# Order of the gate's second choice, the expert sums and the next tile's projections in a fused attention and expert layer

## The chip, the cores and the metric

One Trainium2 chip, one of its cores. The metric is the device time of one execution in microseconds. The kernel before has a median of 419.21 us over 3 runs (419.05 to 419.9).

## The reference, cut to what matters

4096 tokens (4 sequences of 1024) of width 128, all in float32. A linear attention with running sums and 16 heads of 8, then a layer norm, an FFN of 512 with gelu, a layer norm, a residual and layer norm, and then eight experts that share one FFN and differ by a low-rank term:

```python
q = sigmoid(heads(Wq, bq)); k = sigmoid(heads(Wk, bk)); v = heads(Wv, bv)
sink_in = normal / sum((q + EPS) * (cumsum(k) + EPS))
src_out = normal / sum((k + EPS) * (cumsum(q) + EPS))
cons_sink = sum((q + EPS) * (cumsum(k * src_out) + EPS)) / normal
cons_src = clip(sum((k + EPS) * (cumsum(q * sink_in) + EPS)) / normal, -1, 1)
src_comp = exp(cons_src) / cumsum(exp(cons_src)) * normal
kv = cumsum(k outer (v * src_comp))                    # along the tokens
x = (q * sink_in / normal) . kv * sigmoid(cons_sink)
h = layernorm(inputs + x @ Wo + bo)
attn = layernorm(h + gelu(h @ W1 + b1) @ W2 + b2)
x2 = layernorm(inputs + attn)
scores = softmax(x2 @ gate_w.T + gate_b); top_v, top_i = top_k(scores, 2)
for e in range(8):
    gate = count(top_i == e) * top_v.sum()
    inter = x2 @ wi.T + bi + (x2 @ lora_A[e].T) @ lora_B[e].T
    out += gate * (relu(inter) @ wo.T + bo)
out = layernorm(x2 + out)
```

## The kernel before, in words

The tokens are worked in 8 tiles of 512 (`TILES`, `TOK`), four groups of 128 tokens each (`SUB`). Every engine runs one program, written out by hand as a list of calls; semaphores alone tie the programs together, so on each engine an instruction that waits holds up all behind it. A call `step(Tile(s))` does a part of four tiles at once: a = s + 1 (its attention up to piece 3), b = s (the rest of its attention, h, FFN), c = s - 1 (x2, gate, first half of its experts) and d = s - 2 (second half, output). Step -1 and `second_step` come first, steps 1 to 7 follow, then `closing`. In steps 1 to 6 tile a exists, in steps 2 to 7 tile d does.

The attention of a tile (lines 943 to 1043, with PE's lines 327 to 406): `cumulate_q`, `cumulate_k` and two products give head sums on PE (`head_sums`), their inverses are spread by ACT and transposed by PE (`denominators_T`), and the same again gives the conserved sums, `cumulate_e` and `compensation_T`. Out of it comes `values` (DVE, vs = v times the factors, line 1030). SP spreads vs by eight DMAs (`spread_vs`, line 287), one for each piece m, with the eight rows of a head repeated; `outer_product(t, m)` multiplies piece m with k into one of three slots of kv, `cumulate_kv(t, m)` scans it, POOL's `product(t, m)` multiplies the scan with q_fac and PE's `reduce_out(t, m)` sums it up in pO. `q_fac` (`query_factor`) needs `factor_T` through bank pA.

The experts of tile c: `x2_T`, `logits`, `lora_in` (PE, bank pM), 13 small gate steps on DVE (`gate`, line 1068, each waits for the one before it), `masked_lora` (line 1121: u1 is the low-rank input under the first choice's mask, ud under second minus first), `u_T` (line 453: the transposes of u1 and ud on PE, both into pM), `u1T_out` and `udT_out` (ACT), and for each quarter f `inter_base`, `inter1` (with u1T), `relu` (ACT), `inter2` (adds udT's part), `second_relu` (DVE, the sum for both choices), `expert_out`. Quarters 0 and 1 are done in step c + 1, quarters 2 and 3 a step later, when the tile is called d.

ACT's order in the middle of a step is `u1T_out(c)`, `gated_constant(c)`, `seed_x(a)`, `udT_out(c)`, `normalise(d, 3)`, `relu(c, 0)`, `relu(c, 1)`, `normalise(b, 1)`. POOL's order over the end of a step is `product(a, 0)`, `scaled_n2(b)` (needs `normalise(b, 1)`, line 870), and in the next step, where that tile is c, `outer_residual` (line 876), two products, `inverse_std(c, 2)` and products 3 to 7. SP's order is spreads 0 and 1 of tile a, `store(d)` (needs `normalise(d, 3)`, line 294), spreads 2 and 3, and in the next step 4, 5, 6 and 7.

Two-input operations of DVE name their operands' homes in the rows: pA, pB, pO, pY, pG and pM are banks of PSUM, all else lies in SBUF.

Of the kernel before, what the change touches and what calls it, by code (L numbers as in the profile page):

```python
# [52 lines left out]
def wait(eng, sem, value):  # L53

    if value <= 0:
        return
    eng.wait_ge(sem, value)
# [8 lines left out]
def build(nc, x, x_t, att_w, consts, wo_rep, rows, gate_row, ffn_w, moe_w, out):  # L66
    ctx = ExitStack()
    with ctx:
# [136 lines left out]
        def u1_bank(t):  # L205
            return pO if t.n == TILES - 1 else pM
# [119 lines left out]
        def _(pe):  # L326
# [48 lines left out]
            def factor_T(t):  # L375
                pe.wait_ge(facx_ready, t.n + 1)
                pe.wait_ge(qsink_ready, t.n + 1)
                spread_T(pA, fac_x[:, :, :].rearrange("p a b -> p (a b)"), facT_ready)
# [74 lines left out]
            def u_T(t, first_one):  # L453
# [7 lines left out]
                elif first_one:  # L461
                    pe.wait_ge(u1_ready, t.n + 1)
                    pe.wait_ge(ud_ready, t.n + 1)
                else:
                    pe.wait_ge(u1T_ready, t.n + 1)
# [129 lines left out]
            def step(s):  # L595
# [3 lines left out]
                if s.n == 1:  # L599
                    pe.wait_ge(y_free[1], 16)  # L600
                    pe.wait_ge(cmoe_ready, 1)
                if D: inter_base(d, 2); inter1(d, 2); inter_base(d, 3); inter1(d, 3)
                if A: project_q(a)
                if s.n == 1: keep_busy(2, pM)
                if B: reduce_out(b, 1)
                if A: project_k(a)
# [24 lines left out]
                if B: ffn_out(b, 2); ffn_out(b, 3)  # L631
                if C: u_T(c, False)
                if A: factor_T(a)
                if C: inter_base(c, 0); inter1(c, 0); inter_base(c, 1); inter1(c, 1); inter2(c, 0); inter2(c, 1)
# [8 lines left out]
        def _(act):  # L643
# [152 lines left out]
            def step(s):  # L796
# [5 lines left out]
                if D: relu(d, 2)  # L802
                if A: q_out(a)
                if D: relu(d, 3)
                if A: k_out(a)
# [127 lines left out]
        def _(dve):  # L933
# [266 lines left out]
            def step(s):  # L1200
# [20 lines left out]
                if C: gate(c, 9)  # L1221
                if A: source(a); k_times_cum_q(a, 1); cumulate_source(a)
                if C: gate(c, 10)
                if A: q_times_cum_k(a, 1)
                if C: gate(c, 11)
                if D: expert_residual(d)
                if A: conserved(a); clip_source(a)
                if C: gate(c, 12); masked_lora(c, True)
                if A: prefix_e(a)
                if C: masked_lora(c, False)  # L1230
                if A: inverse_cum_e(a); source_factor(a); sink_factor(a)
                if D: piece_moments(d, 3)
                if A: values(a)
                if D: join_moments(d, 3)
                if B: moments(b, 1)
                if A: query_factor(a); outer_product(a, 0); cumulate_kv(a, 0)
                if A: outer_product(a, 1)
                if C: second_relu(c, 0); second_relu(c, 1)
                if A: outer_product(a, 2); cumulate_kv(a, 1); outer_product(a, 3); cumulate_kv(a, 2)
# [53 lines left out]
```

## Time and profile before

| | us |
|---|---|
| median of 3 runs | 419.21 (419.05 to 419.9) |
| the profiled execution | 418.39 |
| its span, first to last instruction | 416.6 |
| PE busy (matmul), weight loads | 374.6, 261.3 |
| DVE busy | 327.9 |
| ACT busy | 216.6 |
| POOL busy | 223.2 |
| mean granted clock of TensorE | 0.99 of full speed |
| chain that ended last | PE 31%, DVE 27%, POOL 19%, issue 14%, DMA 5% |

The shares are means over the start, six steps that look alike and a closing part. A step is read best by itself: the one taken here begins with DVE's `cumulate_q` at 178.56 and ends at 222.89. In it tile a is tile 4. PE is the matmul side; its times are modelled, so a busy PE needn't be at its peak. "Idle before" is the time in which an engine sat idle ahead of the instruction, and behind the arrow stands what ended it.

### The profile page before, as it was taken

What the parts mean: (1) busy time and instruction counts of PE and PEld (TensorE: products, weight loads), DVE (VectorE), ACT (ScalarE), POOL (GpSimd) and SP (SyncE); (2) the same over time, 40 slices, a digit from 0 to 9 for tenths busy, and PEclk for the clock granted to TensorE, in tenths of its full rate; (3) what the DMA queues carried; (4) which work ended last, traced back from release to release, by engine and by line L of the source; (5) the groups of instructions that cost most, each with busy time, mean ns of one, the idle gap of its engine ahead of it and who ended that gap; (6) DMA issues with size and microseconds to landing.
All of it is one profiled execution on the core that took longest, in us unless ns stands there. A gap on an engine that the chain in (4) does not pass through costs nothing.

```text
span 416.6 us, 6454 instructions
## 1 busy us (share of the span) xinstructions
PE 374.6 (90%) x2082; PEld 261.3 (63%) x2082; DVE 327.9 (79%) x787; ACT 216.6 (52%) x399; POOL 223.2 (54%) x263
## 2 busy tenths in 40 slices
PE   8897789788998999989998999899989997799991
PEld 3555556465756875677657774778478765775551
DVE  3649966599589988999799979997899889832632
ACT  2240226327853586538852795278644874175541
POOL 2017234983279527963497348942795369735211
PEclk9999999899999999999999999999999999999997
DMA  8236006400180007300560028000810063000000
GB/s 257 115 71 158 1 2 152 125 3 0 37 217 2 0 2 183 97 0 2 116 162 2 0 56 223 3 0 16 204 36 0 2 160 68 0 1 27 12 14 25
DMA packets 19857, 26.58 MB, mean 64 GB/s; under 512 B 1648, under 2 KB 9968, under 8 KB 19824
## 3 DMA queue, kind: packets, MB, share of 16 engines
q1 hardware_dynamic: 19680, 25.96, 24.5%
q8 instruction: 17, 0.28, 0.3%
q10 hardware_dynamic: 144, 0.21, 0.3%
q14 instruction: 16, 0.13, 0.1%
HBM read 7.29 MB, written 2.10 MB: 23 GB/s over the span
## 4 chain that ended last, share of the span: by engine, by line
PE 31%; DVE 27%; POOL 19%; issue 14%; DMA 5%; ACT 2%; SPq 0%; POOLq 0%; DVEq 0%; ACTq 0%
POOL prod L848 12%; PE pB L354 5%; DMA vb<-vs 5%; DVE kv L1037 5%; PE pY L428 4%; PE pG L421 3%; DVE cum_kv L1043 3%; DVE cum_ks L937 2%; PE pG L497 2%; POOL rstd L838 2%; PE pG L490 2%; DVE cum_q L937 2%; PE pY L508 2%; DVE cum_qs L937 2%; DVE gel L1141 2%
## 5 line engine op out<-in xcount | busy, mean ns | idle before, releaser
L848 POOL TENSOR_TENSOR prod<-cum_kv,q_fac 128x512 f32<-128x512 f32 x64 | 94.5, 1483 | 33.9 <-DVE cum_kv L1043 25.7
L404 PEld LDWEIGHTS pO<-s_wor,prod 128*128 128x128 f32 x512 | 62.2, 191 | 33.5 <-POOL prod L848 21.4
L404 PE MATMUL pO<-s_wor,prod 128*128 128x128 f32 x512 | 69.5, 281 | 14.0 <-POOL prod L848 13.9
L1037 DVE TENSOR_TENSOR kv<-k,vb 128x512 f32<-128x512 f32 x64 | 52.8, 825 | 6.7 <-DMA vb<-vs 6.7
L835 POOL TENSOR_TENSOR var_eps<-mv,s_con 128x4 f32<-128x4 f32 x32 | 9.9, 310 | 71.1 <-DVE mv L1063 71.1
L1043 DVE TENSOR_TENSOR_SCAN cum_kv<-p_ones,cum_kv,kv 128x512 f32<-128x512 f32 x32 | 40.5, 1275 | 0.6
L1043 DVE TENSOR_TENSOR_SCAN cum_kv<-p_ones,kv 128x512 f32<-128x512 f32 x32 | 38.5, 1213 | 0.5
L657 ACT ACTIVATE v<-pA,s_att 128x512 f32<-128x512 f32 x7 | 4.8, 687 | 62.9 <-PE pA L340 62.9
L754 ACT ACTIVATE relu<-pG,s_att 128x512 f32<-128x512 f32 x28 | 19.2, 684 | 27.4 <-PE pG L490 27.4
L508 PEld LDWEIGHTS pY<-s_moe,gel 128*128 128x128 f32 x256 | 30.7, 192 | 3.7 <-issue 1.9
L508 PE MATMUL pY<-s_moe,gel 128*128 128x128 f32 x256 | 32.6, 276 | 0.0
L838 POOL TENSOR_TENSOR rstd<-var_eps,s_con 128x4 f32<-128x4 f32 x32 | 32.5, 1014 | 0.0
L428 PE MATMUL pY<-s_ffn,gel 128*128 128x128 f32 x256 | 32.3, 276 | 0.0
L428 PEld LDWEIGHTS pY<-s_ffn,gel 128*128 128x128 f32 x256 | 30.4, 192 | 1.0 <-ACT pY L723 0.5
L421 PE MATMUL pG<-hT,s_ffn 128*128 128x512 f32 x64 | 30.5, 598 | 0.2
L484 PE MATMUL pG<-x2T,s_moe 128*128 128x512 f32 x60 | 30.6, 594 | 0.0
L490 PE MATMUL pG<-u1T,s_moe 128*128 128x512 f32 x60 | 30.5, 592 | 0.0
L497 PE MATMUL pG<-udT,s_moe 128*128 128x512 f32 x60 | 29.5, 605 | 0.0
L1141 DVE SCALAR_TENSOR_TENSOR gel<-pG,neg_bi,relu 128x512 f32<-128x512 f32 x28 | 20.3, 744 | 10.6 <-PE pG L497 10.5
L891 POOL TENSOR_TENSOR e_norm<-esrc,s_con 128x64 f32<-128x64 f32 x8 | 2.8, 346 | 40.8 <-ACT esrc L684 40.8
L354 PEld LDWEIGHTS pB<-s_att,kq 128*128 128x128 f32 x128 | 16.0, 191 | 12.5 <-issue 9.6
L712 ACT ACTIVATE gel<-pG,s_att 128x512 f32<-128x512 f32 x32 | 21.9, 685 | 2.8 <-PE pG L421 2.5
(164 smaller groups left out, 772.7 us busy)
## 6 DMA issues: line engine op xcount, KB each, us to landing
vb<-vs SPq DMA_DIRECT2D x64, 256.0 KB, 4.7
xT<-x_t SPq DMA_DIRECT2D x8, 256.0 KB, 4.3
xt<-x SPq DMA_DIRECT2D x8, 256.0 KB, 5.3
out<-y SPq DMA_DIRECT2D x8, 256.0 KB, 2.3
s_moe<-moe_w SPq DMA_DIRECT2D x1, 836.0 KB, 10.4
s_wor<-wo_rep SPq DMA_DIRECT2D x1, 512.0 KB, 8.2
s_ffn<-ffn_w SPq DMA_DIRECT2D x1, 512.0 KB, 8.9
s_con<-consts SPq DMA_DIRECT2D x1, 502.0 KB, 4.4
```

Source lines behind the costliest of these rows:

```text
L354: mm = pe.matmul(pB[:, end - P:end], src[:, s * P:(s + 1) * P], wide_sum, start=True, stop=True)
L404: mm = pe.matmul(pO3[:, s, :], prod[:, m % 4, s * P:(s + 1) * P], s_wor[:, m, :], start=False, stop=(m == DH - 1), skip_group_check=True)
L421: pe.matmul(pG[f % 2][:, :], w1[:, f * P:(f + 1) * P], hT[:, :], start=True, stop=True).then_inc(w1_done, 1)
L428: mm = pe.matmul(pY3[:, s, :], gel[:, f, s * P:(s + 1) * P], w2[:, f, :], start=False, stop=(f == FC - 1), skip_group_check=True)
L484: pe.matmul(expert_bank(t, f)[:, :], moe("wi")[:, f * P:(f + 1) * P], x2T[t.par][:, :], start=True, stop=False)
L490: pe.matmul(expert_bank(t, f)[:, :], moe("lb")[:, f * P:(f + 1) * P], u1T[:, :], start=False, stop=True).then_inc(in1_done, 1)
L497: pe.matmul(expert_bank(t, f)[:, :], moe("lb")[:, f * P:(f + 1) * P], udT[:, :], start=False, stop=True, skip_group_check=True).then_inc(i ...
L508: mm = pe.matmul(pY3[:, s, :], hsum[:, f, s * P:(s + 1) * P], wo[:, f, :], start=(f == 0 and s == 0), stop=(f == FC - 1), skip_group_check ...
L838: pool.tensor_tensor(rstd[i][:, :], var_eps[i][:, :], con("mhalf"), ALU.pow).then_inc(rstd_ready[i], 1)
L848: pool.tensor_tensor(prod[:, m % 4, :], cum_kv[t.par][:, m, :], q_fac[t.par][:, :], ALU.mult).then_inc(prod_ready, 1)
L1037: dve.tensor_tensor(kv[:, m % 3, :], k[t.par][:, :], vb[:, m, :], ALU.mult).then_inc(kv_ready, 1)
L1043: dve.tensor_tensor_scan(cum_kv[t.par][:, m, :], scan_ones, kv[:, m % 3, :], start, ALU.mult, ALU.add).then_inc(cumkv_ready, 1)
```

## The change

On DVE, gate step 9 goes from behind `cumulate_sink` to behind the moments of tile d, ahead of `values`; steps 10, 11 and 12 and ud's mask go behind `values`. The moments of d are joined earlier, `sink_factor` comes ahead of `source_factor`, and `cumulate_kv(a, 1)` ahead of the two `second_relu(c, ...)`. On PE, the first choice's transposes go into bank pA instead of pM, so they don't wait for ud any more but for q_sink of the tile two further on; `factor_T` waits for u1T, and stands with `inter_base(c, 0)` and `inter1(c, 0)` ahead of the transposes of ud. `project_q` and `project_k` stand at the head of a step, ahead of tile d's inner matmuls, and ACT's `q_out` and `k_out` ahead of its relus. The programs of SP and POOL are the same.

```diff
--- before.py
+++ after.py
@@ -203,7 +203,7 @@
             return prod[:, f, :] if t.n == TILES - 1 else relu1[:, f % 2, :]
 
         def u1_bank(t):
-            return pO if t.n == TILES - 1 else pM
+            return pO if t.n == TILES - 1 else pA
 
         p_den, p_cons, p_cume = pB[:, SUMS_AT:SUMS_AT + 2 * HW], pB[:, CONS_AT:CONS_AT + 2 * HW], pB[:, 0:HW]
         p_log = pM[:, LOG_AT:LOG_AT + SUB * EXPERTS].rearrange("p (s e) -> p s e", s=SUB)
@@ -375,6 +375,7 @@
             def factor_T(t):
                 pe.wait_ge(facx_ready, t.n + 1)
                 pe.wait_ge(qsink_ready, t.n + 1)
+                wait(pe, u1T_ready, t.n - 1)
                 spread_T(pA, fac_x[:, :, :].rearrange("p a b -> p (a b)"), facT_ready)
 
             def cumulate_e(t):
@@ -460,9 +461,12 @@
                         pe.wait_ge(ud_ready, t.n + 1)
                 elif first_one:
                     pe.wait_ge(u1_ready, t.n + 1)
+                    if t.plus(2).exists():
+                        pe.wait_ge(qsink_ready, t.n + 3)
+                    else:
+                        pe.wait_ge(qfac_ready, TILES)
+                else:
                     pe.wait_ge(ud_ready, t.n + 1)
-                else:
-                    pe.wait_ge(u1T_ready, t.n + 1)
                 for s in range(SUB):
                     mm = pe.transpose(dst[:, s * P:(s + 1) * P], src[:, s, :], ident)
                 mm.then_inc(done, 1)
@@ -599,11 +603,10 @@
                 if s.n == 1:
                     pe.wait_ge(y_free[1], 16)
                     pe.wait_ge(cmoe_ready, 1)
+                if A: project_q(a); project_k(a)
+                if s.n == 1: keep_busy(2, pM)
                 if D: inter_base(d, 2); inter1(d, 2); inter_base(d, 3); inter1(d, 3)
-                if A: project_q(a)
-                if s.n == 1: keep_busy(2, pM)
                 if B: reduce_out(b, 1)
-                if A: project_k(a)
                 if D: inter2(d, 2); inter2(d, 3)
                 if B: reduce_out(b, 2)
                 if s.n == 1: keep_busy(1, pM)
@@ -629,9 +632,10 @@
                 if B: ffn_out(b, 1)
                 if A: compensation_T(a)
                 if B: ffn_out(b, 2); ffn_out(b, 3)
+                if A: factor_T(a)
+                if C: inter_base(c, 0); inter1(c, 0)
                 if C: u_T(c, False)
-                if A: factor_T(a)
-                if C: inter_base(c, 0); inter1(c, 0); inter_base(c, 1); inter1(c, 1); inter2(c, 0); inter2(c, 1)
+                if C: inter_base(c, 1); inter1(c, 1); inter2(c, 0); inter2(c, 1)
                 if A: reduce_out(a, 0)
             opening(Tile(0))
             second_step(Tile(0))
@@ -799,10 +803,8 @@
                 A, B, C, D = a.exists(), b.exists(), c.exists(), d.exists()
                 if s.n == 1:
                     act.wait_ge(cmoe_ready, 1)
-                if D: relu(d, 2)
-                if A: q_out(a)
-                if D: relu(d, 3)
-                if A: k_out(a)
+                if A: q_out(a); k_out(a)
+                if D: relu(d, 2); relu(d, 3)
                 if C: normalise(c, 2); x2T_out(c)
                 if A: v_out(a)
                 if C: gate_exp(c)
@@ -1218,25 +1220,23 @@
                 if C: gate(c, 4); gate(c, 5); sum_exp(c)
                 if C: gate(c, 6); gate(c, 7); gate(c, 8); inverse_sum_exp(c); gate_total(c)
                 if A: sink(a); cumulate_sink(a)
-                if C: gate(c, 9)
                 if A: source(a); k_times_cum_q(a, 1); cumulate_source(a)
-                if C: gate(c, 10)
                 if A: q_times_cum_k(a, 1)
-                if C: gate(c, 11)
                 if D: expert_residual(d)
                 if A: conserved(a); clip_source(a)
-                if C: gate(c, 12); masked_lora(c, True)
+                if C: masked_lora(c, True)
                 if A: prefix_e(a)
-                if C: masked_lora(c, False)
-                if A: inverse_cum_e(a); source_factor(a); sink_factor(a)
                 if D: piece_moments(d, 3)
+                if A: inverse_cum_e(a); sink_factor(a); source_factor(a)
+                if D: join_moments(d, 3)
+                if C: gate(c, 9)
                 if A: values(a)
-                if D: join_moments(d, 3)
+                if C: gate(c, 10); gate(c, 11); gate(c, 12); masked_lora(c, False)
                 if B: moments(b, 1)
                 if A: query_factor(a); outer_product(a, 0); cumulate_kv(a, 0)
-                if A: outer_product(a, 1)
+                if A: outer_product(a, 1); cumulate_kv(a, 1)
                 if C: second_relu(c, 0); second_relu(c, 1)
-                if A: outer_product(a, 2); cumulate_kv(a, 1); outer_product(a, 3); cumulate_kv(a, 2)
+                if A: outer_product(a, 2); outer_product(a, 3); cumulate_kv(a, 2)
                 if B: moments(b, 2)
             step(Tile(-1))
             second_step(Tile(0))
```

## Rows read from the trace of the kernel before

**Rows 1.** Windows of one step: columns us, busy us and instructions by engine, clock, DMA.

```profile
178.56:222.89 44.33, 41.94 (x251) 30.79 (x251) 40.37 (x100) 27.19 (x50) 27.85 (x32) 1.00 0.27 66
```

**Rows 2.** DVE's timeline: start us, us, line, operation, out<-in, count, idle before.

```profile
190.46 1.33 DVE L957 SCALAR_TENSOR_TENSOR kq<-k,cum_qs 128x512 f32<-128x512 f32 x1
...
192.84 0.15 DVE L1098 TENSOR_REDUCE m_pick<-pick 128x4 f32<-128x32 f32 x1
192.95 0.69 DVE L964 SCALAR_TENSOR_TENSOR qk<-q,cum_ks 128x512 f32<-128x512 f32 x1
```

**Rows 3.** POOL's timeline, same step.

```profile
189.97 1.27 POOL L868 TENSOR_TENSOR h_res<-h_res,r_b1b 128x512 f32<-128x512 f32 x1
...
208.15 1.30 POOL L874 TENSOR_TENSOR res<-n,s_row 128x512 f32<-128x512 f32 x1 [0.71 <-ACT n L700]
209.52 1.59 POOL L879 TENSOR_TENSOR res<-res,x_b2n 128x512 f32<-128x512 f32 x1
...
223.05 1.26 POOL L848 TENSOR_TENSOR prod<-cum_kv,q_fac 128x512 f32<-128x512 f32 x1 [0.21 <-DVE cum_kv L1043]
```

**Rows 4.** The chain of waits in the middle of the step: start us, us, what.

```profile
199.89 0.70 DVE vs L1032
200.61 3.15 DMA vb<-vs
```

**Rows 5.** PE's timeline, this step and the start of the next.

```profile
193.70 1.16 PE L354 MATMUL pB<-s_att,qk 128*128 128x128 f32 x8 [0.43 <-DVE qk L964]
...
201.48 0.60 PE L467 MATMUL pM<-s_con,ud 128*128 128x128 f32 x4
...
202.35 1.02 PE L484 MATMUL pG<-x2T,s_moe 128*128 128x512 f32 x2
...
205.79 2.07 PE L497 MATMUL pG<-udT,s_moe 128*128 128x512 f32 x4
...
227.47 1.13 PE L354 MATMUL pB<-s_att,kq 128*128 128x128 f32 x8 [0.18 <-DVE kq L957]
```

**Rows 6.** ACT's timeline, middle of the step.

```profile
202.30 0.59 ACT L750 ACTIVATE udT<-pM 128x512 f32<-128x512 f32 x1
202.78 1.64 ACT L700 ACTIVATE y<-res,shift,rstd 128x128 f32<-128x128 f32 x4
204.32 0.68 ACT L754 ACTIVATE relu<-pG,s_att 128x512 f32<-128x512 f32 x1
205.99 0.69 ACT L754 ACTIVATE relu<-pG,s_att 128x512 f32<-128x512 f32 x1 [0.99 <-PE pG L490]
206.57 1.50 ACT L700 ACTIVATE n<-pY,shift,rstd 128x128 f32<-128x128 f32 x4
```

**Rows 7.** DVE's timeline, behind the values.

```profile
204.51 1.22 DVE L1043 TENSOR_TENSOR_SCAN cum_kv<-p_ones,kv 128x512 f32<-128x512 f32 x1
205.65 0.67 DVE L1037 TENSOR_TENSOR kv<-k,vb 128x512 f32<-128x512 f32 x1
206.85 0.75 DVE L1141 SCALAR_TENSOR_TENSOR gel<-pG,neg_bi,relu 128x512 f32<-128x512 f32 x1 [0.53 <-PE pG L497]
...
208.56 1.43 DVE L1037 TENSOR_TENSOR kv<-k,vb 128x512 f32<-128x512 f32 x1
```

**Rows 8.** SP's queue of DMAs, behind the values.

```profile
204.45 0.39 SPq L296 DMA_DIRECT2D out<-y  x1
204.88 4.50 SPq L292 DMA_DIRECT2D vb<-vs  x5
```

**Rows 9.** All spreads of vs (line 292): from issue to landing.

```profile
DMA to landing us min/median/max: 3.1/4.7/6.3
```

**Rows 10.** PE's timeline in step 7.

```profile
373.47 0.60 PE L467 MATMUL pM<-s_con,ud 128*128 128x128 f32 x4
...
377.34 2.07 PE L497 MATMUL pG<-udT,s_moe 128*128 128x512 f32 x4
```

**Rows 11.** ACT's timeline in step 1.

```profile
115.21 0.69 ACT L754 ACTIVATE relu<-pG,s_att 128x512 f32<-128x512 f32 x1 [1.38 <-PE pG L490]
```

## The prediction, made before the changed kernel was run

> **What bounds the kernel now.** I read the windows of one step first: DVE is busy 40.37 of 44.33 us, PE 41.94, at a granted clock of 1.00; ACT and POOL have room [rows 1]. With two engines nearly full, what counts is where each waits. So I followed the chain of waits through this step (it begins at 178.56) and then laid the four engines' timelines beside it. Three stretches follow one another.
>
> (a) From the spread denominators to `values`: DVE in its own order up to `q_times_cum_k(a,1)`, then PE in its own order. PE is idle 0.43 us until DVE's qk is there at 193.70, and works off its queue from there to `compensation_T` and `values` [rows 4, 5].
>
> (b) From `values` (199.89) through the spread by DMA (3.15 us) to the outer products, expert sums and POOL's products, until product 7 ends at 223.05 + 1.26 = 224.31 [rows 3, 4].
>
> (c) PE's queue behind product 7: `reduce_out(b,7)`, `expert_out(d,0)`, `project_v`, then `head_sums` at 227.47. In front of it PE idled only 0.18 us, for DVE's kq [rows 5]. So the products may end some 0.2 us later before the head sums are later, and a faster DVE alone wins no more than about as much.
>
> **The change part by part,** in the times of this step.
>
> Gate steps 9 to 12. Steps 9 and 10 stood ahead of qk. From step 10 to qk is 192.95 - 192.84 = 0.11 us, and that comes off the chain [rows 2]. Step 9 stood ahead of `k_times_cum_q(a,1)`, which takes 1.33 us, about twice the 0.69 of qk, beside POOL's h_res, which ends at 189.97 + 1.27 = 191.24: it can end only some 0.55 us after that, so starting it 0.11 earlier wins nothing [rows 2, 3]. I take 0.11 (bounds 0.1 and 0.25; the upper if both count). Steps 11, 12 and ud lay beside PE's queue and win nothing there. Behind `values` three gate steps and ud come to at most 3 x 0.22 + 0.69 = 1.35 us, bounded by qk's duration for ud; they lie beside the DMA of 3.15 us, which also covers `moments(b,1)` and q_fac. I cost them at nothing; without that cover they'd cost up to 0.3. The swap of `sink_factor` and `source_factor` moves one small instruction inside DVE's wait for PE: nothing. `values` is thus at 199.78.
>
> First choice's transposes in pA. The new waits (q_sink read, u1T read) are over long before: nothing. What counts is `u_T(c,False)`, now behind `factor_T`, `inter_base(c,0)` and `inter1(c,0)`. The four pairs between 202.35 and 205.79 take 0.86 us each; `factor_T`, four transposes like those of ud, takes 202.35 - 201.48 = 0.87 for both groups, 0.43 for one [rows 5]. So ud's group starts at 201.48 - 0.11 + 0.43 + 1.72 = 203.52, ends after its 0.60, and ACT's `udT_out` starts near 204.15, not 202.30. ACT's order stays, so all that is queued behind it moves: `normalise(d,3)` + 0.48, `relu(c,0)` + 1.54, that is 206.17, `relu(c,1)` at 206.76, `normalise(b,1)` + 0.58 at 207.35, against 206.57 [rows 6]. Before, ACT idled 0.99 ahead of `relu(c,1)`; of the new wait of 1.85 us this absorbs all but 0.78, the 0.11 of the gates counted in.
>
> Who waits for that:
> - PE: `inter2(c,0)` needs `relu(c,0)`, done at 206.85, and starts at 206.9 instead of 205.79: 1.1 us later [rows 5, 6]. Within a step PE gets it back where it now waits for POOL's products.
> - DVE: the `second_relu(c,...)` come 1.1 us later (207.95 for 206.85). `cumulate_kv(a,1)`, now in front, a scan of 1.22, takes about that long, so the idle 0.53 stays as it is and nothing is won or lost [rows 7].
> - POOL: `scaled_n2` starts at 208.93 instead of 208.15, and products 1 to 7 stand behind it and `outer_residual` [rows 3].
> - SP: the store of tile d waits for `normalise(d,3)`, now done 1.85 later, and the spreads of pieces 2 and 3 stand behind the store: from 206.7 instead of 204.88 [rows 8]. At 3.1 to 4.7 us to landing (the first of a burst lands soonest), piece 2 is there at about 210.1 and piece 3 near 211.4, where DVE wants them at 209.75 and 210.4 [rows 9].
>
> So `outer_product(a,2)` waits to about 210.2 and `outer_product(a,3)`, which meets POOL's `outer_residual` running from 210.3 on, to about 211.9. The pattern is in the row of 1.43 us: a kv, 0.67 a little earlier, starts at 208.56 beside POOL's 208.15 to 209.45 and ends at 209.99, so its real work is from 209.3 on; and the POOL instruction behind takes 1.59, not 1.30 [rows 3, 7]. The two don't run side by side.
>
> The Trainium skill says the same of the pair of ports that both engines share (SBUF — State Buffer, "Who interferes with whom"), and adds that whoever issues first has it for the whole instruction. By that rule `outer_residual` goes ahead of `outer_product(a,3)` and product 7 ends 0.75 us late; in the other order it would be 0.6. The rows agree on the exclusion and show no case in which both stand waiting.
>
> Sum of (b): with DVE 0.7 to 0.9 late at `moments(b,2)`, product 7 ends at about 224.95 for 224.31. Lower bound + 0.15: POOL alone is 0.78 late and has waits of 0.21 for DVE before each of products 5 to 7 to give back [rows 3]. Upper bound + 1.1, the DMA later by another 0.5. I take + 0.65, nearest to the row of 1.43. Less the slack of 0.2 in (c) it is 0.45 a step, bounds 0 and 0.9 (the gates' 0.11 is already in it); since POOL's waits may give part of it back I go by + 0.35.
>
> The projections ahead of the inner matmuls: q and k are needed only by the next step's scans. `relu(d,2)`, `relu(d,3)` and the `second_relu(d,...)` behind them come two pairs, 1.7 us, later, and are needed only behind those scans too. Nothing; without that cover at most the 1.7. The warm-up matmuls of step 1 only move.
>
> Where it counts in full. Steps 2 to 5 give 4 x 0.35 = 1.4 us. Step 1 has no tile d, so neither `normalise(d,3)` nor a store, and ACT waited 1.38 us ahead of `relu(c,0)`, which takes in the later ud [rows 11]: - 0.1. Step 6 ends in the last tile's products, with nothing in (c) to hide behind: + 0.6. In step 7 `inter2(c,0)` starts at 377.34, and PE goes on from it without a stop. `u_T(c,False)` goes from 373.47 to 375.2; by ACT's distances above (0.63, 0.48, 1.54, and 0.7 for the relu) `inter2` starts at 378.6: + 1.25 us, all of it to the end [rows 6, 10]. Sum: 1.4 - 0.1 + 0.6 + 1.25 = 3.15 us. On the profiled execution's 418.39 us that is 421.5; on the median of 419.21, 0.8 above it, 422.4.
>
> **The rivals.**
> 1. DVE's filled wait wins: faster. The place is `cumulate_kv(a,1)` ahead of the expert sums, the price the idle 0.53 and the long kv of 1.43. For it: DVE is 91% busy [rows 1]. Against: it decides only if `normalise(b,1)` comes less than 0.4 us late, and ACT's order says 0.78. POOL then gives back up to 3 x 0.21, about 0.5 a step, six times 3 us: 416.2.
> 2. POOL alone decides (the lower bound): product 7 + 0.15, inside the slack of 0.2, so steps 2 to 5 change by nothing or - 0.05, step 6 by + 0.15, and the tail's 1.25 stays, less 0.1 to 0.3: 420.2. For it: DVE's own time sums up no longer than before. Against: the row of 1.43.
> 3. The DMA decides: slower still. The store's 256 KB and the spreads behind it push pieces 4 to 7 as well, and steps 2 to 6 pay 0.9 each: 4.5 + 1.25 + 0.3 = 6.1: 425.3. Here belongs a lower clock from PE's longer stop; the rows have 1.00 granted throughout this step and give it no price [rows 1].
>
> **How the numbers follow.** Forecast 0.65 (422.4), rival 1 0.12, rival 2 0.16, rival 3 0.07. The range, 419.7 to 425.0, takes in rival 2 but its lowest part, and the step's bounds up to 0.65 with 1.3 more in the last step and the tail; it leaves out rival 1, most of rival 3 and a little, two in ten. A measurement of this kernel tells 0.2%, 0.84 us, from no change. Faster is rival 1, 0.12; same is half of rival 2 and a low edge of the forecast, 0.12; slower the rest, 0.76.
>
> **What would show it.** Right: `udT_out` near 2 us behind its old place with ACT idle ahead of it; `relu(c,0)` right behind `normalise(d,3)`; `inter2(c,0)` waiting about 1.1 us for ACT; the store and the spreads of pieces 2 and 3 issued 1.8 us later; kv waiting for DMA at piece 2 or 3, not only at piece 0; product 7 ending 0.3 us or more later behind `values` than the present 24.42; a tail 1.2 us longer. Wrong: products that end sooner behind `values`; `normalise(b,1)` at its old distance; head sums that wait for DVE alone. The forecast falls if ACT gets ud sooner than PE's order says, or if POOL catches up.

## The result, and the profile after

| | before | after |
|---|---|---|
| median | 419.14 us (418.63 to 419.93) | 425.74 us (425.22 to 427.17) |
| ratio, 95% interval | | 1.0161 (1.0141 to 1.018) |
| the profiled execution | 418.39 | 425.68 |
| its span | 416.6 | 423.9 |

The change makes the kernel 1.6% slower. The prediction was slower by 0.8%, 422.4 with a range up to 425.0: the direction was right, the size was half of what came, and the time lies outside the range. The two profiled executions differ by 7.3 us of span. The start of `values` (vs) for tiles 0 to 7 shows where they go:

```
tile      0      1       2       3       4       5       6       7
before  25.48  63.47  110.83  155.28  199.89  244.33  288.98  333.44
after   25.53  65.39  112.74  157.15  202.56  247.85  293.26  338.54
later    0.05   1.92    1.91    1.87    2.67    3.52    4.28    5.10
```

So 1.9 us are lost between tiles 0 and 1, in the opening (in the two executions that were profiled; more on that under e1 and e4); nothing in step 1 (tile 2 to 3, -0.04); 0.80, 0.85, 0.76 and 0.82 in steps 2 to 5; and behind the values of tile 7 another 2.2, of which product 7 of that tile takes 0.77 (it ends 25.50 us behind vs, for 24.73) and the tail behind it 1.43.

The same step as in the rows of before begins at 181.22 now. The window of it, columns as in [rows 1]: 45.18 us long for 44.33, with PE and DVE busy for as long as before. It is all waiting.

```profile
181.22:226.40 45.18, 41.88 (x250) 30.88 (x251) 40.48 (x100) 27.27 (x50) 27.90 (x32) 1.00 0.26 65
```

ACT's timeline of after, behind vs at 202.56 (before: [rows 6], vs at 199.89). udT_out has a wait of 1.90 in front of it and starts 4.38 behind vs, for 2.41; the normalise for `normalise(b,1)` starts 7.55 behind, for 6.68.

```profile
206.94 0.60 ACT L754 ACTIVATE udT<-pM 128x512 f32<-128x512 f32 x1 [1.90 <-PE pM L471]
207.43 1.64 ACT L704 ACTIVATE y<-res,shift,rstd 128x128 f32<-128x128 f32 x4
208.97 1.24 ACT L758 ACTIVATE relu<-pG,s_att 128x512 f32<-128x512 f32 x2
210.11 1.50 ACT L704 ACTIVATE n<-pY,shift,rstd 128x128 f32<-128x128 f32 x4
```

Who waits for it, on SP, PE and POOL: the spreads of pieces 2 and 3 are issued from 6.97 behind vs (4.99 before, [rows 8]), inter2 waits 1.17 for ACT's relu, scaled_n2 starts 9.13 behind vs (8.26, [rows 3]) and product 7 ends at 227.83, 25.27 behind vs (24.42).

```profile
209.53 4.48 SPq L292 DMA_DIRECT2D vb<-vs  x5
...
209.79 1.96 PE L501 MATMUL pG<-udT,s_moe 128*128 128x512 f32 x4 [1.17 <-ACT relu L758]
...
211.69 1.29 POOL L876 TENSOR_TENSOR res<-n,s_row 128x512 f32<-128x512 f32 x1 [1.59 <-ACT n L704]
...
226.56 1.27 POOL L850 TENSOR_TENSOR prod<-cum_kv,q_fac 128x512 f32<-128x512 f32 x1 [0.21 <-DVE cum_kv L1045]
```

DVE in the same stretch (before: [rows 7]). The scan of piece 1 now fills time ahead of the expert sums, but 0.69 of idle are left, and then pieces 2 and 3 both wait for their DMA, and the outer product of piece 3 takes 0.86 beside POOL's `outer_residual` (213.06 to 214.68), for 0.69 of that of piece 2. The scan of piece 2 starts 12.59 behind vs; before it was 211.63 - 199.89 = 11.74. That is 0.85.

```profile
209.01 1.22 DVE L1045 TENSOR_TENSOR_SCAN cum_kv<-p_ones,kv 128x512 f32<-128x512 f32 x1
210.93 1.61 DVE L1143 SCALAR_TENSOR_TENSOR gel<-pG,neg_bi,relu 128x512 f32<-128x512 f32 x2 [0.69 <-PE pG L501]
212.86 0.69 DVE L1039 TENSOR_TENSOR kv<-k,vb 128x512 f32<-128x512 f32 x1 [0.32 <-DMA vb<-vs]
214.36 0.86 DVE L1039 TENSOR_TENSOR kv<-k,vb 128x512 f32<-128x512 f32 x1 [0.81 <-DMA vb<-vs]
215.15 1.21 DVE L1045 TENSOR_TENSOR_SCAN cum_kv<-p_ones,kv 128x512 f32<-128x512 f32 x1
```

And PE at the next head sums: 28.42 behind vs for 27.58, and the wait in front of them is the same 0.18, for the same kq [rows 5].

```profile
230.98 1.13 PE L354 MATMUL pB<-s_att,kq 128*128 128x128 f32 x8 [0.18 <-DVE kq L959]
```

The opening, which the prediction did not look at. DVE and POOL of before, and then of after:

```profile
36.62 0.68 DVE L1037 TENSOR_TENSOR kv<-k,vb 128x512 f32<-128x512 f32 x1
37.22 2.32 DVE L1043 TENSOR_TENSOR_SCAN cum_kv<-p_ones,kv 128x512 f32<-128x512 f32 x2
...
36.59 1.82 POOL L848 TENSOR_TENSOR prod<-cum_kv,q_fac 128x512 f32<-128x512 f32 x1
```

```profile
36.78 1.78 DVE L1039 TENSOR_TENSOR kv<-k,vb 128x512 f32<-128x512 f32 x1
38.49 2.32 DVE L1045 TENSOR_TENSOR_SCAN cum_kv<-p_ones,kv 128x512 f32<-128x512 f32 x2
...
36.76 1.26 POOL L850 TENSOR_TENSOR prod<-cum_kv,q_fac 128x512 f32<-128x512 f32 x1 [1.76 <-DVE cum_kv L1045]
39.78 2.48 POOL L850 TENSOR_TENSOR prod<-cum_kv,q_fac 128x512 f32<-128x512 f32 x2 [1.76 <-DVE cum_kv L1045]
...
41.09 2.90 PE L405 MATMUL pO<-s_wor,prod 128*128 128x128 f32 x16 [1.86 <-POOL prod L850]
43.89 2.04 PE L354 MATMUL pB<-s_att,kq 128*128 128x128 f32 x8
```

With scan 1 ahead of outer product 2, POOL has finished product 1 and stands ready when scan 2 is done; it starts product 2 at 36.76, and DVE's outer product 4, 0.02 us later, takes 1.78 instead of 0.68. Before, POOL's product 2 also started ahead of outer product 4, by 0.03 (36.59 and 36.62), but there it was POOL that was held up, with 1.82 for the 1.26 of now. So one of the two stands in both kernels, and the start times don't tell which. With DVE standing, scans 3 and 4 are 1.27 later, PE stands 1.86 for product 3, and the granted clock, 1.00 from 40 to 50 before, is 0.78 and then 0.88 there (windows, columns as in [rows 1]); the head sums of tile 1 take 2.04 for 1.13.

```profile
40.00:45.00 5.00, 3.84 (x21) 3.49 (x22) 4.97 (x7) 0.00 (x0) 2.26 (x2) 0.78 0.00 0
45.00:50.00 5.00, 5.00 (x30) 4.04 (x30) 4.08 (x5) 2.06 (x4) 1.26 (x1) 0.88 0.00 0
```

### The profile page after: what moved, and what is told of

The parts are those of the page before. It is cut to its first block, busy times and chain, and to the rows that moved or that the text cites. A ratio compares the mean times of both kernels' runs of the same rounds, so it can differ in the third digit from the quotient of the medians.

```text
span 423.9 us, 6454 instructions
## 1 busy us (share of the span) xinstructions
PE 374.1 (88%) x2082; PEld 262.7 (62%) x2082; DVE 330.8 (78%) x787; ACT 216.6 (51%) x399; POOL 222.9 (53%) x263
## 4 chain that ended last, share of the span: by engine, by line
PE 29%; DVE 25%; POOL 18%; issue 17%; DMA 6%; ACT 4%; SPq 0%; POOLq 0%; DVEq 0%; ACTq 0%
POOL prod L850 13%; PE pB L354 6%; DMA vb<-vs 6%; PE pY L429 4%; DVE kv L1039 4%; PE pG L422 3%; DVE cum_kv L1045 3%; DVE cum_ks L939 2%; POOL rstd L840 2%; PE pY L512 2%; DVE cum_qs L939 2%; DVE gel L1143 2%; DVE cum_q L939 2%; DVE rden L971 2%; POOL res L876 2%
## 5 line engine op out<-in xcount | busy, mean ns | idle before, releaser
L405 PEld LDWEIGHTS pO<-s_wor,prod 128*128 128x128 f32 x512 | 63.5, 193 | 32.4 <-POOL prod L850 17.9
```

The lines of the kernel that those rows point to most:

```text
L405: mm = pe.matmul(pO3[:, s, :], prod[:, m % 4, s * P:(s + 1) * P], s_wor[:, m, :], start=False, stop=(m == DH - 1), skip_group_check=True)
```

## The experiments

The theory with which they began: the loss per step and that of the tail come from one thing, ACT's udT_out, which waits for PE's later transposes and stands ahead of `normalise(d,3)` and the relus; the 1.9 of the opening come from the scan of piece 1 in step -1. The rivals: the store and the spreads behind it (rival 3 of the prediction) make the per-step loss; the later gates and mask make it; or rival 1, the filled wait, is a gain that something else covers up. Later ones ask why a step lost 0.8 rather than 0.35, and what a step could gain. Each ratio is to runs of the kernel before beside it on the same chip.

**e1_opening, e2_scan_first: the scan of the opening, taken out of the change, and put alone into before.**

```diff
 # e1, from after. e2, from before: the scan early for tile 0, late for the others
-                if A: outer_product(a, 1); cumulate_kv(a, 1)
+                if A: outer_product(a, 1)
+                if A and a.n > 0: cumulate_kv(a, 1)
                 if C: second_relu(c, 0); second_relu(c, 1)
-                if A: outer_product(a, 2); outer_product(a, 3); cumulate_kv(a, 2)
+                if A: outer_product(a, 2)
+                if A and a.n == 0: cumulate_kv(a, 1)
+                if A: outer_product(a, 3); cumulate_kv(a, 2)
```

> The changed kernel, with the scan of piece 1 back behind outer product 2 in step -1 alone (tile 0). Theory: the first 1.9 us of the loss (vs of tile 1 at 65.39 us for 63.47) come from that one call: kv of piece 4 starts 0.02 us behind POOL's product 2, waits it out, DVE is 1.3 us late, PE pauses longer and runs at a lower granted clock from 40 to 50 us. Then 425.7 - 1.9 = 423.8 us, vs of tile 1 back at 63.5, granted clock 1.00 from 40 to 50. Rival: the 1.9 us are the luck of one profile (loads landing later): 425.7, or the start varies without it.

> The kernel before, with the scan of piece 1 ahead of outer product 2 in step -1 alone. Theory as above: 419.1 + 1.9 = 421.0 us, a longer kv of piece 4 and a lower clock from 40 to 50 us. Rival: 419.1.

Measured: e1 424.19 (423.6 to 425.8), ratio 1.0131 (1.0101 to 1.0161); e2 420.23 (419.82 to 421.64), ratio 1.0037 (1.0024 to 1.005), which is 1.7 us. From the values of tile 0 to those of tile 1, e2 takes 39.55 us, before 37.99. The rows of e2 have the same pair as after, again 0.02 apart:

```profile
36.53 1.78 DVE L1037 TENSOR_TENSOR kv<-k,vb 128x512 f32<-128x512 f32 x1
...
36.51 1.26 POOL L848 TENSOR_TENSOR prod<-cum_kv,q_fac 128x512 f32<-128x512 f32 x1 [1.76 <-DVE cum_kv L1043]
```

In e1 this stretch of DVE, POOL and the head sums is as before (outer product 4 takes 0.68), but its profiled execution had a granted clock of 0.83 from 50 to 60, and took 38.84 from tile 0 to tile 1. Three other kernels of this study have the same 0.83 there with that stretch as before (e7, e8 and e10), and six have 1.00 (e3, e5, e6, e9, e11, e12). The kernel before has its 0.83 later, from 75 to 85, where it costs nothing: 47.36 from tile 1 to tile 2, and 47.35 in e11, with 1.00 in both stretches.

The opening isn't safe without the early scan either. e4 below has e1's scan order, and its profiled execution has the long outer product all the same, with POOL's start again 0.02 ahead; with 0.83 from 50 to 60 on top it took 39.92 from tile 0 to tile 1, as long as the changed kernel.

```profile
36.46 1.26 POOL L850 TENSOR_TENSOR prod<-cum_kv,q_fac 128x512 f32<-128x512 f32 x1
...
36.48 1.78 DVE L1039 TENSOR_TENSOR kv<-k,vb 128x512 f32<-128x512 f32 x1
```

Of the twelve profiled executions with the scan in its old place, e4's is the only one in which DVE stood there; with the scan early DVE stood in both (after and e2). So the early scan costs 1.7 by the medians of e2 against before; taken out of the change (e1) it gives back less, 0.9 by the distances from before (5.7 for 6.6), and the single times of e1, from 423.6 to 425.8, lie wide. Some 0.8 us of clock and at times the 1.1 of the outer product come and go in an execution's opening without an edit; what decides either is open.

**e3_act_order: udT_out behind the normalise and the first relu.**

```diff
                 # e1, and on ACT:
-                if C: udT_out(c)
                 if D: normalise(d, 3)
-                if C: relu(c, 0); relu(c, 1)
+                if C: relu(c, 0); udT_out(c); relu(c, 1)
                 if B: normalise(b, 1)
```

> As e1_opening, and ACT takes udT_out behind normalise(d,3) and relu(c,0) instead of ahead of them. Theory: what a step pays is ACT's wait for ud and what is queued behind it. normalise(b,1) then starts 0.9 us sooner (7.55 us behind vs now, 6.7 then), inter2(c,0) doesn't wait, piece 2 doesn't wait for its DMA, and steps 1 to 6 are as long as before the change, the tail too: 419.2 us (418.6 to 420.2). Rival, that the loss is DVE's order (gate steps and ud behind the values): 423 us, with product 7 still 25.2 us behind vs.

Measured: 418.74 (418.05 to 421.35), ratio 1.0005 (0.9987 to 1.0022). One place in ACT's order gives back 5.4 us, all of the per-step loss and the tail; steps 2 to 5 take 44.40 to 44.54 between values, as before. All else of the change but the opening's scan is still in it and together is worth nothing that the interval could show. ACT's timeline, with vs at 199.98: no wait in front of udT any more, and `normalise(b,1)` 6.69 behind vs.

```profile
202.39 1.65 ACT L704 ACTIVATE y<-res,shift,rstd 128x128 f32<-128x128 f32 x4
203.93 0.69 ACT L758 ACTIVATE relu<-pG,s_att 128x512 f32<-128x512 f32 x1
204.51 0.59 ACT L754 ACTIVATE udT<-pM 128x512 f32<-128x512 f32 x1
206.08 0.69 ACT L758 ACTIVATE relu<-pG,s_att 128x512 f32<-128x512 f32 x1 [0.98 <-PE pG L494]
206.67 1.50 ACT L704 ACTIVATE n<-pY,shift,rstd 128x128 f32<-128x128 f32 x4
```

**e4_store: the spreads ahead of the store.**

```diff
                 # e1, and on SP:
-                if D: store(d)
                 if A: spread_vs(a, 2); spread_vs(a, 3)
+                if D: store(d)
```

> As e1_opening, and SP issues the store of tile d behind the spreads of pieces 2 and 3. kv of pieces 2 and 3 then can't wait for the store. Theory that the late normalise(b,1) and the exclusion of DVE's and POOL's two-input operations decide: kv of piece 2 waits for POOL's scaled_n2 and kv of piece 3 for outer_residual instead, scan 2 starts where it did: 423.8 us, product 7 at 25.3 behind vs. Rival, that the DMA decides: 0.5 us less in each of five steps, 421.3 us.

Measured: 424.89 (424.19 to 425.54), ratio 1.0136 (1.0108 to 1.0165). Steps 2 to 5 still take 45.27 to 45.40. The pieces are there in time now, and DVE waits for POOL in the place of the DMA: its outer products 2 and 3 together take 2.76, and the scan of piece 2 starts 214.96 - 202.39 = 12.57 behind vs, as in after.

```profile
212.28 2.76 DVE L1039 TENSOR_TENSOR kv<-k,vb 128x512 f32<-128x512 f32 x2
214.96 1.21 DVE L1045 TENSOR_TENSOR_SCAN cum_kv<-p_ones,kv 128x512 f32<-128x512 f32 x1
```

So with the DMA out of the way POOL alone makes the same delay: the DMA was a second wait beside it, and not what decides. Rival 3 falls as a cause.

**e5_ud_order_only: PE's late transposes of ud put alone into before.**

```diff
-                if C: u_T(c, False)
                 if A: factor_T(a)
-                if C: inter_base(c, 0); inter1(c, 0); inter_base(c, 1); ...   # cut at the right
+                if C: inter_base(c, 0); inter1(c, 0)
+                if C: u_T(c, False)
+                if C: inter_base(c, 1); ...
```

> The kernel before with one edit on PE: the transposes of ud stand behind factor_T, inter_base(c,0) and inter1(c,0). Gates, masks, scans, projections, ACT and SP are those of before. Theory (PE's late transposes are sufficient): udT_out starts 1.9 us later behind values, normalise(b,1) 0.9 to 1.0 later, product 7 ends 0.7 to 0.9 later behind values, the last tile costs 1.4 more: 419.2 + 6 x 0.8 + 1.4 = 425.4, between 424.2 and 425.8. Rival (it takes the later mask on DVE, gates and ud behind values, as well): under 421. The opening stays as before, the values of tile 1 as early as there.

Measured: 424.71 (423.76 to 424.94), ratio 1.0134 (1.0119 to 1.0149), as much as e1. The transposes alone are sufficient for the per-step loss and the tail, and e3 shows that ACT's order is what turns them into it. The later gates and mask are not needed for it. (The step from tile 1 to tile 2 is 0.44 shorter in this trace, 46.92 for 47.36: a product of POOL and an outer product of DVE start 0.06 apart there, at 80.54 and 80.60, and DVE takes 0.66, where in before it took 1.76 at the same distance.)

**e6_scan_only: rival 1 by itself.** The edit is that of e1's scan order, put into before in every step but the first.

> The kernel before with one edit on DVE: cumulate_kv(a,1) stands ahead of the two second_relus in every step but the first. This is rival 1 of the prediction by itself, with nothing late. Rival 1: DVE's idle 0.53 and 0.29 are filled and each step is 0.5 us shorter: 416.2. The theory of now: the scan fills the wait, but piece 3 is then multiplied beside POOL's outer_residual instead of behind it, takes 1.4 instead of 0.66 us and gives it all back: the scan of piece 2 ends 12.9 us behind values as before, 419.2 within 0.4.

Measured: 418.12 (417.64 to 418.7), ratio 0.9984 (0.9973 to 0.9996), -0.8 us in all and not the -3 of rival 1. The two waits of 0.53 and 0.29 [rows 7] are gone, and the two outer products behind take 2.88 together for 1.43 and 0.66, since both now meet POOL's `scaled_n2` and `outer_residual`. With vs at 199.44 `moments(b,2)` starts at 12.84, for 12.87 before.

```profile
207.04 1.38 DVE L1141 SCALAR_TENSOR_TENSOR gel<-pG,neg_bi,relu 128x512 f32<-128x512 f32 x2
208.34 2.88 DVE L1037 TENSOR_TENSOR kv<-k,vb 128x512 f32<-128x512 f32 x2
...
207.69 1.30 POOL L874 TENSOR_TENSOR res<-n,s_row 128x512 f32<-128x512 f32 x1 [0.71 <-ACT n L700]
209.08 1.60 POOL L879 TENSOR_TENSOR res<-res,x_b2n 128x512 f32<-128x512 f32 x1
```

**e7_gates_only: gate steps 9 to 12 alone, each one place later, none ahead of qk.** (From before.)

```diff
-                if C: gate(c, 9)
                 if A: source(a); k_times_cum_q(a, 1); cumulate_source(a)
-                if C: gate(c, 10)
                 if A: q_times_cum_k(a, 1)
-                if C: gate(c, 11)
+                if C: gate(c, 9)
                 if D: expert_residual(d)
+                if C: gate(c, 10)
                 if A: conserved(a); clip_source(a)
-                if C: gate(c, 12); masked_lora(c, True)
+                if C: gate(c, 11)
+                if C: masked_lora(c, True); gate(c, 12)
```

> The kernel before with gate steps 9 to 12 one place later each, none of them ahead of q_times_cum_k(a,1). The prediction's step: the values come 0.11 us earlier in each step, 6 x 0.11 = 0.7: 418.5. The theory of now: qk waits for the end of the cum_ks scan, beside which the small gate step lay, so nothing is gained: head sums to values 16.86 as before, 419.2 within 0.3.

Measured: 422.48, from 420.19 to 424.11, ratio 1.0083 (1.0049 to 1.0118). Neither expectation holds: it is slower, and it scatters. The profiled execution was the shortest, 420.19; it has four of its last five distances between values at 44.45 to 44.64, as before, and one, from 200.59 to 246.12, at 45.53. In that one DVE's small scan `prefix_e` takes 1.40; a step earlier it takes 0.28, and in all steps of before 0.26 to 0.31. Here are that scan and POOL's `x_bo` in the two steps:

```profile
241.26 1.40 DVE L1019 TENSOR_TENSOR_SCAN e_pref<-s_con,esrc 128x64 f32<-128x64 f32 x1
...
241.24 1.27 POOL L853 TENSOR_TENSOR x_bo<-xt,s_row 128x512 f32<-128x512 f32 x1
...
196.86 0.28 DVE L1019 TENSOR_TENSOR_SCAN e_pref<-s_con,esrc 128x64 f32<-128x64 f32 x1
...
196.85 1.36 POOL L853 TENSOR_TENSOR x_bo<-xt,s_row 128x512 f32<-128x512 f32 x1
```

Before, the scan started at 196.03 and POOL's instruction at 196.15, 0.12 behind. One gate step more ahead of the scan has used up that lead: POOL's start is now 0.01 to 0.02 ahead in every step from tile 2 on, and in this execution DVE passed in five of them and stood 1.1 us in one. That the slower executions of e7 are those in which it stood more often fits their spread, but only the fastest one has a trace, so it isn't shown. In the changed kernel, whose last gate steps go behind the values, the scan keeps a lead (198.59 for POOL's 198.82) and never stands.

The Trainium skill has the rule for such a pair (SBUF — State Buffer, "Who interferes with whom"): a DVE instruction with two inputs in SBUF contends with a POOL instruction that reads SBUF, and the order of issue decides who blocks. The rows agree that one of the two is held up (1.40 for 0.28, or POOL's 1.36 for 1.27). Who came first they don't show here: the starts lie 0.02 apart where DVE stood and 0.01 where it passed, POOL's ahead in both, and in the opening above DVE passed at 0.03 and stood at 0.02.

Now to the 0.11 that this run was made for. In before, qk doesn't start behind the gate step but behind the end of the scan in front of that. A step later in before, and then the same place in after: 236.03 + 1.27 is 237.30, and qk is at 237.34; in after, with no gate step between, 239.55 + 1.27 is 240.82 and qk is at 240.86.

```profile
236.03 1.27 DVE L937 TENSOR_TENSOR_SCAN cum_ks<-p_ones,cum_ks,k_src 128x512 f32<-128x512 f32 x1
237.22 0.16 DVE L1098 TENSOR_REDUCE m_pick<-pick 128x4 f32<-128x32 f32 x1
237.34 0.69 DVE L964 SCALAR_TENSOR_TENSOR qk<-q,cum_ks 128x512 f32<-128x512 f32 x1
```

```profile
239.55 1.27 DVE L939 TENSOR_TENSOR_SCAN cum_ks<-p_ones,cum_ks,k_src 128x512 f32<-128x512 f32 x1
240.86 0.69 DVE L966 SCALAR_TENSOR_TENSOR qk<-q,cum_ks 128x512 f32<-128x512 f32 x1
```

**e11_dve_delay, e12_pool_delay: has stage (c) any slack?**

```diff
 # both from before: e11 on DVE, e12 on POOL; in each, delay is one of the last two lines
-                if B: moments(b, 2)
+                if B: delay(b); moments(b, 2)
...
-                if B: product(b, 3); product(b, 4); product(b, 5); product(b, 6); product(b, 7); shifted_x(b)
+                if B: product(b, 3); product(b, 4); product(b, 5); product(b, 6); delay(b); product(b, 7); shifted_x(b)
...
+                dve.reciprocal(spare[:, t.n % 2, :], p_ones[:, 0:P])
+                pool.tensor_tensor(spare[:, t.n, :], row("g2"), row("g2"), ALU.mult)
```

> The kernel before with one more instruction of DVE, a reciprocal of 128x128 of about 0.9 us whose output nothing reads, ahead of moments(b,2) in steps 1 to 7. The prediction's slack of 0.2: values of the next tile come 0.7 us later a step. The theory of now (DVE runs without a pause from the scan of piece 2 to kq, so it passes on all of its lateness): 0.87 to 0.9 a step, seven steps: 425.0 to 425.5, and head_sums still waits 0.18 for kq.

> The kernel before with one more instruction of POOL, a product of 128x128 of 0.35 to 0.5 us whose output nothing reads, ahead of product(b,7) in steps 1 to 7. POOL's wait of 0.21 for cum_kv takes in part of it and the 0.18 that PE waits for DVE's kq takes in the rest: the values of the next tile come 0 to 0.1 later a step, 419.2 to 419.9. If POOL's product 7 were what carries the step, 0.15 to 0.3 a step: 420.2 to 421.

Measured: e11 422.14 (422.05 to 423.1), ratio 1.0078 (1.0063 to 1.0093), 0.65 to 0.71 a step; e12 419.3 (418.45 to 419.63), ratio 1.0005 (0.9994 to 1.0016), 0.05 to 0.11 a step. POOL's 0.39 us more per step are all but swallowed: its wait of 0.21 is gone, product 7 ends 24.52 behind vs for 24.42, and the head sums still wait for kq, which takes 0.88 for 0.78 beside a POOL instruction that starts 0.1 later. That is the 0.1 that is left.

```profile
223.62 0.39 POOL L878 TENSOR_TENSOR spare<-s_row 128x128 f32<-128x128 f32 x1
223.98 1.26 POOL L849 TENSOR_TENSOR prod<-cum_kv,q_fac 128x512 f32<-128x512 f32 x1
```

e11 gave the number of the expectation that I thought the wrong one (0.7), so it had to be read in the trace. The extra instruction moves `moments(b,2)` by 0.85; the statistics take 0.80 for 0.84, and the outer product of piece 4 behind them 0.66 for 0.80, as it no longer meets POOL. So 0.66 are left at scan 3, and from there to kq nothing is given back: kq starts 27.31 behind vs for 26.65, and PE waits 0.18 for it. For DVE the wait isn't slack: it is DVE's own instruction that ends it.

```profile
214.80 0.93 DVE L1136 RECIPROCAL spare<-p_ones 128x128 f32<-128x128 f32 x1
...
216.79 0.66 DVE L1038 TENSOR_TENSOR kv<-k,vb 128x512 f32<-128x512 f32 x1
...
230.17 1.13 PE L355 MATMUL pB<-s_att,kq 128*128 128x128 f32 x8 [0.18 <-DVE kq L958]
```

**e8_piece2_early, e9_before_piece2, e10_no_store_swap: what the step can gain.** If DVE's lateness at `moments(b,2)` passes on, DVE's earliness should too, up to POOL's limit. e3, e4 and e6 show the place: outer products 2 and 3 against POOL's scaled_n2 and outer_residual. Piece 2 can be multiplied before POOL's pair and piece 3 behind it, if piece 2 has landed.

```diff
                 # DVE, steps from 0 on, as in e9 and e10 (from before); step -1 keeps the old order.
                 # e8 comes to the same order from after, with e3's edit on ACT
                 if A: outer_product(a, 1)
+                if A: cumulate_kv(a, 1); outer_product(a, 2)
                 if C: second_relu(c, 0); second_relu(c, 1)
-                if A: outer_product(a, 2); cumulate_kv(a, 1); outer_product(a, 3); cumulate_kv(a, 2)
+                if A: cumulate_kv(a, 2); outer_product(a, 3)
                 # SP, e8 and e9 only
-                if D: store(d)
                 if A: spread_vs(a, 2); spread_vs(a, 3)
+                if D: store(d)
```

> The changed kernel with the opening's scan back, udT_out behind normalise(d,3) and relu(c,0) on ACT, the store behind the spreads of pieces 2 and 3 on SP, and in every step but the first outer_product(a,2) ahead of the two second_relus and cumulate_kv(a,2) ahead of outer_product(a,3). So neither product of DVE meets scaled_n2 or outer_residual of POOL. Theory (what passes to the next step is when DVE is through with pieces 2 and 3): DVE is 1.2 us earlier at moments(b,2); POOL, whose waits of 0.21 ahead of products 5 to 7 are all it can give back, lets 0.6 of it through: 6 x 0.6, 415.6, between 415 and 417. Rival (DVE's time there isn't what counts, or piece 2 isn't landed at 7.6 us behind values): 419.2.

> The kernel before with two edits: the store behind the spreads of pieces 2 and 3 on SP, and in every step but the first DVE's order outer products 0, 1, scan 1, outer product 2, the two second_relus, scan 2, outer product 3. Gates, masks, transposes, projections are those of before. If nothing of the change is worth anything here, it runs as the version before it in this study (product 7 ends 23.4 us behind values): 412.9, within 0.8. If the later gates or the mask bring part of that gain, it is slower: 414 or more.

> As e9_before_piece2, but with SP's order of before: the spreads of pieces 2 and 3 wait behind the store, are issued 4.99 us behind values and land no sooner than 8.1, where DVE wants piece 2 at 6.2. DVE stands about 1.9 us in front of outer_product(a,2), the second_relus behind it. Theory (spread order is needed for the gain): DVE begins moments(b,2) between 12.1 and 13.2 us behind values, for 12.87 before: 416.5 to 420. Rival (the order on DVE alone does it): 413.

Measured: e8 412.94 (412.46 to 413.05), ratio 0.9853 (0.9837 to 0.987); e9 412.71 (412.45 to 412.89), ratio 0.9848 (0.9833 to 0.9862); e10 417.13 (416.61 to 417.92), ratio 0.9959 (0.9945 to 0.9974). e9 is the version that beats both kernels: before with two reorderings, 6.3 us less, and with nothing of the change in it. e8 has the gates, mask, transposes and projections of the change and the same time. In e9, vs at 198.13, outer product 2 starts at 205.70, 0.69 ahead of POOL's scaled_n2 at 206.39, and outer product 3, at 208.74, meets only the end of outer_residual (207.76 to 209.02):

```profile
205.70 0.67 DVE L1037 TENSOR_TENSOR kv<-k,vb 128x512 f32<-128x512 f32 x1
...
208.74 0.84 DVE L1037 TENSOR_TENSOR kv<-k,vb 128x512 f32<-128x512 f32 x1
...
217.19 1.74 DVE L1037 TENSOR_TENSOR kv<-k,vb 128x512 f32<-128x512 f32 x1
```

`moments(b,2)` starts 11.37 behind vs (12.87 before), product 7 ends 23.41 behind (24.42), and the steps take 43.43 to 43.55, 1.0 to 1.1 less. I had let through 0.6, counting only POOL's waits of 0.21; POOL also begins product 1 earlier, and its outer_residual takes 1.26 for 1.59 with outer product 3 behind it. Of the 1.5 that DVE is early at `moments(b,2)` only 1.0 reach kq (25.63 behind vs for 26.65): outer product 7, the last row above, now takes 1.74 for 0.67, with POOL's product 5 started 0.08 ahead of it, while outer product 5 takes 0.67 for 1.12. So even e9 has a stand left in each step; no run takes it out. In e10, with the store in front of the spreads, piece 2 is waited for (0.62), and DVE comes to it 0.03 behind POOL:

```profile
207.84 1.78 DVE L1037 TENSOR_TENSOR kv<-k,vb 128x512 f32<-128x512 f32 x1 [0.62 <-DMA vb<-vs]
...
207.81 1.26 POOL L874 TENSOR_TENSOR res<-n,s_row 128x512 f32<-128x512 f32 x1 [0.72 <-ACT n L700]
```

That is tile 4. For tiles 3 and 5 outer product 2 starts 0.01 to 0.03 ahead of POOL's `scaled_n2` and takes 0.69, and POOL's instruction 1.81 and 1.83. The steps from values to values, from tile 2 on, are 43.42, 44.12, 44.47, 44.14 and 44.49. So without the order on SP the order on DVE brings 1.9 of the 6.3 us. SP's order put alone into before was not run; in e4 it gave nothing.

## Why the prediction was right or wrong, point by point

- **udT_out near 2 us late, and all behind it.** Right to a few hundredths: 4.38 behind vs for the 4.37 worked out, `normalise(b,1)` 7.55 for 7.57, the spreads 6.97 for 6.92, scaled_n2 9.13 for 9.15, inter2 waiting 1.17 for "about 1.1". e3 and e5 show that the per-step and the tail loss come from this.
- **The gates' 0.11.** Wrong. The small instruction lay in the time in which qk waits for the scan's end anyhow; head sums to values take 16.86 before and 16.87 after. I read the difference of two starts as a cost, where only the end of the instruction that qk depends on counted.
- **Product 7 at + 0.65.** Too small. It ends 0.85 later, 25.27 behind vs. Of the 0.20, 0.11 are the gates. The other 0.09 are the pair of outer product 3 and outer_residual. With outer_residual ahead, as in the prediction's sentence on the Trainium skill (SBUF — State Buffer, "Who interferes with whom"), the 0.75 with the gates' 0.11 taken out are 0.86, and 0.85 was measured; the trace has that order, outer_residual from 213.06 and outer product 3 from 214.36. That the number fits so well is in part luck, since outer product 3 was also held by its DMA up to 214.36. The kernel of e4, in which the DMA isn't late, comes to the same 12.57 through POOL alone.
- **The slack of 0.2 in (c).** Of the steps of the argument this one failed most, with the opening below. I took the 0.18 that PE waits for kq as room for POOL, and it is; but the lateness doesn't come by POOL. From the scan of piece 2 on, DVE has no pause up to kq, so it hands on all of its delay, and POOL's products 5 to 7 wait the same 0.21 for it as before. The sentence "a faster DVE alone wins no more" read one side only. e12 shows the slack for POOL, e11 and the unchanged 0.18 show none for DVE.
- **+ 0.45, gone by as + 0.35,** for what POOL's waits might give back. They give back nothing, as POOL waits for DVE. The steps came to 0.81 on average: 0.35, and 0.11 (gates), 0.09 (the pair), 0.20 (slack), 0.10 (this) make 0.85. The four steps of the 1.4 lost 3.23, a miss of 1.8.
- **The opening at nothing.** Wrong by 1.9, the other half. The scan moves in step -1 too, where no expert sums stand to be filled in, and there DVE's outer product 4 and POOL's product 2 start 0.02 to 0.03 apart, before and after; with the early scan it was DVE that stood, 1.1 us, and the granted clock fell behind it (0.78 and 0.88). The prediction went through the steps in which a tile c exists and never asked what the line does in step -1. e2 gives 1.7 for it alone; e4 shows that the same stand can come without it.
- **Step 1, - 0.1, and step 6, + 0.6:** measured - 0.04 and + 0.77. **The tail, + 1.25:** 1.43; udT_out waits 3.08 there, and inter2 has its 1.17.
- **Projections, first choice's transposes, swap of the factors at nothing:** right. With the opening and ACT's order mended, the rest of the change leaves 1.0005 (e3), and e8 and e9, with and without it, agree.
- **Rival 1,** the filled wait: e6 gives 0.8 of its 3 us. The two idle times do go; POOL's pair takes them back. **Rival 3** named about the right time (425.3) for the wrong reason, a DMA that decides: in e4 it doesn't. **Rival 2** (POOL alone) had the wait but the wrong carrier.
- **The sum:** 3.15 + 1.8 + 1.9 + 0.2 (tail) + 0.2 (step 6) + 0.1 (step 1) is 7.35, for the 7.3 by which the spans differ.

## What to carry to other kernels

A wait in front of the consumer is slack only for the engine that isn't named in it: follow the named engine back through its own queue, and if it runs there without a pause, every delay put into it comes out at the end. When an instruction moves in a list that all steps share, read the first and the last step as well as the middle one. And look for long instructions of DVE and POOL that overlap, above all for pairs that start within a few hundredths of each other: a neutral reordering lost 1.1 us a time at such a pair (e2, e7), and e9, which keeps outer products 2 and 3 all but clear of POOL's pair, is 6.3 us faster.

## What the runs showed of the hardware that was not expected

- When long instructions of DVE and POOL with their inputs in SBUF start within some 0.03 us of each other, one of the two is held up, and the start times of the trace don't say which. With POOL's start 0.02 to 0.03 ahead DVE stood in after, e2 and e4 (1.78, POOL 1.26), in one step of e7 (1.40 for 0.28) and in e10 (1.78), and it passed in before (0.68, POOL 1.82) and in the openings of the other runs; at 0.06, behind the opening, it stood in before (1.76) and passed in e5 (0.66). With the scan of `prefix_e` 0.12 ahead of POOL it passed in all steps of before.
- The long scans, one of whose operands (`p_ones`) is a bank of PSUM like those listed ahead of the rows, run at 1.21 to 1.28 beside POOL in all of these rows.
- The profile books such a stand as duration of the instruction that is held up, not as idle time, so the list of waits doesn't show it: it is seen only as one row longer than its siblings.
- A small instruction between a scan and the instruction that needs its result costs nothing: qk starts 0.04 us behind the scan's end with it and without it.
- The granted clock of the opening stretch from 50 to 60 us was 0.83 in some profiled executions and 1.00 in others whose engines did the same up to there, worth 0.8 us of the first tile. Why, the runs here don't tell.
